# Turning tiles by fp32 products with the identity instead of TensorE's transpose mode, in a two-layer graph and attention kernel

## The reference, cut to what matters

```python
xn = _layernorm(x)
x = x + gnn0(xn, edges) + linear_attention0(xn)        # layer 0: mean over neighbours, relu attention
x = x + gqa(_layernorm(x))                             # 8 heads, 625 x 625 scores, softmax
xn = _layernorm(x)
x = x + gnn1(xn, edges) + linear_attention1(xn)        # layer 1: gathered messages, softmax attention
x = x + anchors_ffn(_layernorm(x))                     # 128 anchors, one 512 x 512 matrix each
```

## Time and profile before

| | us |
|---|---|
| median of 3 runs | 2634.62 |
| lowest and highest run | 2627.95, 2638.78 |
| profiled execution, its own time | 2621.18 |
| span of the profiled execution | 2619.2 |

### The profile page before, as it was taken

How to read it: one execution, slowest core, us unless ns; L and a number is a source line. 1 busy time by engine, 2 the same in 40 slices (tenths; PEclk the granted TensorE clock), 3 DMA queues, 4 the chain that set the end, 5 groups by cost and what they waited for, 6 DMA issues and landing times.

```text
span 2619.2 us, 34595 instructions
## 1 busy us (share of the span) xinstructions
PE 2457.5 (94%) x11680; PEld 2056.2 (79%) x11680; DVE 1802.2 (69%) x2675; ACT 924.4 (35%) x1128; POOL 1649.6 (63%) x724
## 2 busy tenths in 40 slices
PE   6989978976899679999999999999999999999999
PEld 6878877865799667777777777777777777777777
DVE  8974324547588657777777777777777777777775
ACT  3732224522389552223223232223222322322231
POOL 0024322228888745777777777777777777777773
PEclk9989877988799779999999999999999999999999
DMA  3024010011433200221212212122122221221211
GB/s 77 16 68 162 17 65 17 1 49 47 110 87 92 79 38 33 97 84 76 96 64 96 95 65 96 69 91 96 64 96 80 80 96 64 96 91 69 96 64 36
DMA packets 49889, 190.90 MB, mean 73 GB/s; under 512 B 13300, under 2 KB 17911, under 8 KB 33444
## 3 DMA queue, kind: packets, MB, share of 16 engines
q1 hardware_dynamic: 35728, 177.90, 19.4%
q0 software_dynamic: 13200, 10.75, 1.9%
q10 hardware_dynamic: 900, 1.44, 0.2%
HBM read 177.54 MB, written 12.35 MB: 72 GB/s over the span
## 4 chain that ended last, share of the span: by engine, by line
PE 79%; DVE 10%; POOL 6%; issue 2%; ACT 2%; DMA 1%; SPq 0%; DVEq 0%; ACTq 0%; POOLq 0%
PE PS L1698 25%; PE PS L1700 25%; PE PS L1699 25%; POOL gatW L751 3%; POOL XN L751 2%; PE PS L1776 2%; DVE hotS L1151 1%; POOL gat L751 1%; DVE hotD L1152 1%; DVE negmax L1388 1%; DVE PTl L1405 1%; PE PS L1962 1%; PE PS L1920 0%; PE PS L1963 0%; DVE XN L1115 0%
## 5 line engine op out<-in xcount | busy, mean ns | idle before, releaser
L1648 DVE SCALAR_TENSOR_TENSOR XN<-PS,attn,XN 125x512 f32<-125x512 f32 x1083 | 805.4, 749 | 439.9 <-PE PS L1700 431.4
L789 POOL TENSOR_TENSOR OPl<-TS,OPh 128x1024 fp32r<-128x1024 f32 x256 | 677.5, 2647 | 116.7 <-ACT OPh L1061 116.7
L789 POOL TENSOR_TENSOR OPl<-RAW,OPh 128x1024 fp32r<-128x1024 f32 x192 | 555.2, 2892 | 273.4 <-ACT OPh L1061 273.4
L1698 PE MATMUL PS<-OPh,XTh 128*125 128x512 f32 x1280 | 507.6, 397 | 2.0 <-DVE attn L1602 2.0
L1700 PE MATMUL PS<-OPh,XTl 128*125 128x512 f32 x1280 | 506.1, 395 | 0.0
L1699 PE MATMUL PS<-OPl,XTh 128*125 128x512 f32 x1280 | 503.7, 394 | 0.0
L1061 ACT ACTIVATE OPh<-TS 128x1024 fp32r<-128x1024 f32 x256 | 271.8, 1062 | 530.0 <-PE PS L1700 517.3
L1061 ACT ACTIVATE OPh<-RAW 128x1024 fp32r<-128x1024 f32 x192 | 203.8, 1062 | 579.1 <-PE PS L1700 579.1
L1698 PE MATMUL PS<-OPh,Sh 128*125 128x512 f32 x1024 | 404.3, 395 | 3.1 <-DVE XN L1645 3.1
L1700 PE MATMUL PS<-OPh,Sl 128*125 128x512 f32 x1024 | 403.4, 394 | 0.0
L1699 PE MATMUL PS<-OPl,Sh 128*125 128x512 f32 x1024 | 402.1, 393 | 0.0
(11 more groups left out here) (345 smaller groups left out, 3587.6 us busy)
## 6 DMA issues: line engine op xcount, KB each, us to landing
RAW<-in_values SPq DMA_DIRECT2D x64, 2048.0 KB, 7.5
filters<-filt SPq DMA_DIRECT2D x14, 672.0 KB
fil<-filters SPq DMA_DIRECT2D x11, 840.0 KB
Wraw<-in_ffn SPq DMA_DIRECT2D x4, 1024.0 KB, 5.3
Wraw<-in_L_q SPq DMA_DIRECT2D x2, 1024.0 KB, 5.1
Wraw<-in_L_k SPq DMA_DIRECT2D x2, 1024.0 KB, 8.7
Wraw<-in_L_v SPq DMA_DIRECT2D x2, 1024.0 KB, 7.3
gatW<-nodes,dstI POOLq DMA_INDIRECT x90
```

The lines of the kernel that those rows point to most:

```text
L789: g.tensor_tensor(OPl[:, j], operand_source(j, parity), OPh[:, j].bitcast(F32), ALU.subtract).then_inc(op_lower, 1)
L1648: v.scalar_tensor_tensor(out=XN[:, t], in0=PS[0:P, bank, :], scalar=w, in1=XN[:, t], op0=ALU.mult, op1=ALU.add).then_inc(v_added, 1)
L1698: mm(dst, lh, rh, start=start, stop=False, skip_group_check=resumed)
```

## The change

In the three places where a tile is turned, the call of the transpose mode becomes an ordinary matrix product. The data stays the stationary operand (the one that is loaded as weights) and the identity the moving one. Sizes, buffers, order and semaphores stay as they were.

```diff
@@ transposes(), line 1713: xt0, xt1, xt2, qT2, xt3, outT
-                        ins = nc.tensor.transpose(slot(u)[:, 0, k * P:(k + 1) * P], src[:, j, c], ident[0:P, 0:P])
+                        ins = mm(slot(u)[:, 0, k * P:(k + 1) * P], src[:, j, c], ident[0:P, 0:P], start=True, stop=True)
@@ linear_attention(), line 1859: ct0, ct2
-                            ins = nc.tensor.transpose(slot(u)[:, 0, k * P:(k + 1) * P], ctx[:, t, k * 128:(k + 1) * 128], ident[0:P, 0:P])
+                            ins = mm(slot(u)[:, 0, k * P:(k + 1) * P], ctx[:, t, k * 128:(k + 1) * 128], ident[0:P, 0:P], start=True, stop=True)
@@ attention, line 1920: probT
-                        ins = nc.tensor.transpose(dst, prob[:, turned % 4, tile_columns(t)], ident[0:P, 0:P])
+                        ins = mm(dst, prob[:, turned % 4, tile_columns(t)], ident[0:P, 0:P], start=True, stop=True)
```

## The result

| kernel | runs | median us | lowest and highest | profiled execution |
|---|---|---|---|---|
| before | 7 | 2633.73 | 2626.69, 2638.84 | 2621.18 |
| after | 7 | 2653.68 | 2648.33, 2661.82 | 2657.02 |

The ratio is 1.0084 with a 95% interval of 1.0065 to 1.0103: the change costs 22 us (17 to 27). The forecast was 28 us and 2662; the direction and the range hold, the size was 6 to 8 us too high. Two executions, one of e11 and one of the kernel before beside e8, took 13,495 and 7,133 us and are left out of the ratios.

What follows compares the result with a forecast made beforehand. PE, busy 94% of the span with 79% of the last-ending chain, was taken as the bound. Stage terms summed to 34.9 us, less 7 from the clock, 28: 2649 on the profiled execution, 2662 as median; range 2646 to 2680.

Steps and rivals of the forecast that it cites:

- The price of a piece: Each turned piece becomes two instructions, costing 0.21 us more at the low clock and 0.11 at the high one.
- The rival of the factor four: fp32 product dearer than line 1982 shows: three extra loads, 105 us less 7, giving 2733; chance 0.05.
- The attention: probT's 200 pieces on line 1920: 5.2 + 19.2 - 6.0 = 18.4 us, with 3.4 back from two clock dips.
- cold start: Start of attention: probT's first 5 units run at the low clock, 25 pieces at 0.21, 5.2 us.
- DVE lags less: In attention, 1.4 us of the 6.9 us of waits for a head's last PTl would be swallowed.
- xt2, qT2 and ct2: Layer 1 after attention: PE's and POOL's strands meet with no slack at DVE's edges; 4.5 us, between 1 and 7.
- xt3: Pieces before dist: 12 take 5.1 instead of 2.5 us, less a vanished 1.55 us slot wait; 1.5 us.
- The clock in dist: fp32 products right before dist may leave the clock high, worth up to 5.65 us; 3.5 counted back.
- xt0, ct0, xt1, outT: Other turned stages: 4.0, 3.8, 1.0 (mostly covered by PE's wait for the chosen weights) and 1.7 us.
- faster, by the clock: Rival: full streaming keeps PE's clock high wherever tiles are turned, 40 us back, giving 2622; chance 0.07.
- waits swallow more: Rival: the softmax chain sets attention's pace, probT costs 6 not 18.4, giving 2650; chance 0.12.
- the rows: Pieces on lines 1713 and 1859, all turned stages but probT: 16.5 us less 3.5 of clock, 13.

Runs made afterwards that it cites:

- e11: Kernel before plus 4 filler products nobody reads ahead of each head's attn products, nowhere else: 2626.23 against 2630.79, ratio 0.9975.
- e8: Kernel before plus filler products nobody reads in PE's waits (num0, first probT, each head's attn, xt3, dist): 2605.76 against 2632.50, ratio 0.9897.
- e5: Kernel before, transpose mode kept, with each piece of xt1, xt3 and outT issued ten times: 2678.92 beside 2634.64.
- e6: Changed kernel with each product of xt1, xt3 and outT issued ten times: 2797.41 beside 2634.64 for the kernel before.
- e12: Kernel before with ordinary products in xt2, qT2 and ct2 alone (60 pieces): 2633.82 against 2633.10, ratio 1.0005.
- e2: Kernel before with ordinary products at lines 1713 and 1859 alone (160 pieces), probT left in transpose mode: 2636.32, ratio 1.0022.
- e13: Kernel before with ordinary products in xt0, ct0, xt1, xt3 and outT alone (100 pieces): 2632.41, ratio 1.0009.

## Why the prediction was right, and where not

The signs held but one. PE's count rose to 12040, a head takes 16.9 us, and the granted clock from num0 to ct2 went from 0.80 (308 to 694 us) to 0.82 (320.6 to 727). The gap ahead of POOL's gather, which was to exceed 0.3, stayed at 0.30.

**The price of a piece** held: one instruction more, 0.11 at the high clock (0.109 in probT, 0.117 per piece between e5 and e6 in outT), twice that at the low. The rival of the factor four falls with it; the advice of the Trainium skill to prefer the transpose instruction (Perfetto Trace Analysis, Optimizing Tensor Performance, Transposes) holds in sign, for 0.8%.

**The attention**, the largest term, was right in its sum and off in its parts. The cold start cost 5.3 us against 5.2: a unit there took 1.41 us and takes 2.46. The other 35 units pay 0.54 each, 18.9 against 19.2: a single unit took 0.81 us in the kernel before, and takes 1.35 in the row at 470.98.

```profile
447.92 0.81 PE L1920 MATMUL PS<-ident,prob 125*125 125x125 f32 x5
```

The waits should have swallowed 6.0: POOL's gave 3.8 against 4.6, and the waits for PTl, which should have given 1.4, took 2.4 more. So the step "DVE lags less" had the wrong sign, and the waits gave 1.4 net. The clock made up for it. The whole attention, first in the kernel before, then after:

```profile
420.60:552.60 132.00, 119.69 (x659) 106.53 (x660) 73.87 (x201) 64.11 (x163) 30.93 (x39) 0.84 0.00 1
```

```profile
437.90:585.80 147.90, 137.74 (x860) 126.74 (x861) 75.75 (x201) 65.84 (x163) 30.87 (x39) 0.88 0.00 1
```

By an estimate from these two rows, a granted clock of 0.84 and of 0.88 makes low stretches of 0.16 / 0.5 x 132.0 = 42 us and 0.12 / 0.5 x 147.9 = 35. Less the cold start, 18.1 and 23.3, that is 24 and 12 us: 12 us less at half speed give 6 back, where 3.4 were counted. 5.3 + 18.9 - 1.4 - 6 = 16.8, and 15.9 was measured. A head takes 16.9 us, where I had said 2 more than 14.6. That the attention came out at its price of 15 is thus in part luck: waits 4.6 short, clock 2.6 better.

**xt2, qT2 and ct2** is the step whose mechanism failed: 4.5 predicted, 1.3 (-2 to +5) measured in e12, and in its trace PE's edge products 4.0 us late with the gathers 1.2. The sentence "they meet there with no slack" read a releaser's name on a usual gap as a wait. Its own test was printed beside it, since the same 0.30 stands before nearly every gather.

**xt3** was priced at 1.5 and cost 0.9 to 2.3, so its size held, though the 2.9 of the stage table looks like twice the price. What the price missed is the stride: line 1982, from which the pace came, loads packed weights, and 14 of the 24 instructions of the row at 998.35 ran at the low clock, where the stride costs little. The trace of before could not show it, as the transpose mode hardly pays for the stride.

**The clock in dist** was to give 3.5 and gave nothing in the kernel after, 1.4 us in e2's trace and 1.7 in e13's. In the kernel after the clock did rise at the end of xt3, at 1001.6, and was low again from 1005.0 on, just ahead of dist's first product. e8 shows that 5.8 us are there, but with 47 extra products, 94 instructions, where the change brings 20.

**xt0, ct0, xt1, outT** came out as 3.1, 4.0, 0.2 and 1.8 in the trace, 9.1 against 10.5. Together with xt3 their cost over many runs looks smaller than that (e13: 2.4, at most 8), and why stays open.

The rival **faster, by the clock** needed turned pieces to be what leaves the clock low. e5 says they are not. The rival **waits swallow more** named the right kind of place, but the waits gave less, not more, than the forecast. That the result fell between it and the forecast is the rows' doing, which cost 6 (2 to 9.5) and were priced at 13; layer 1 is about 3 of these 7.

One end of the range is summed wrongly: the low terms (12, 1 and 17) leave 8 us, not about 12, or 11 if hn's 3 us are not counted twice. The measured 22 is far from it.

## What to carry to other kernels

Turn fp32 tiles with the transpose mode: the ordinary product is two instructions with a weight load each, and at the high clock each of them takes twice as long again if the piece has a stride of four. Count such a change in instructions times pace, and take the pace from the distance between starts, at either clock. Where PE's clock is low beside short waits, products that nobody reads, put ahead of the wait on PE's queue, are worth trying: 106 of them gave 1% here.

Before a wait is put on the path, compare its length with the gap before its neighbours. Before a difference of two profiles is explained, look at a stretch that neither kernel edits; and before a stage is called longer, look whether it started at the same point of the work around it.

## What the runs showed of the hardware that I had not expected

- A product with every fourth column as its weights takes 0.23 us per instruction at a granted clock of 1.00, with packed ones 0.11; the transpose mode takes 0.117 with the same stride. At 0.50 it is 0.23 too, against 0.21.
- Turned pieces back to back raise the clock from 0.50 to 1.00 and hold it for 21.55 us, while instructions that stream 32 columns let it fall with PE busy for 79.16 of 80 us.
- In one instruction the load of 128 columns and the stream of 125 take about 0.11 us each; cutting either to a quarter leaves the pace at 0.108.
- The 135 gathers from the end of v2 on, never more than 0.7 us apart, take 248 us in one execution and 259 in another.
- The stretch from the degrees to num0, with the same instructions, takes 112 or 122 us from one execution to another, by its granted clock of 0.97 or 0.87.
